# Down products of two experts on the two column halves of a PSUM bank, added by the turn, in a hybrid attention and expert kernel

## What is computed

```python
def _L2_ffn_ref(x, Wr, br, W1, b1, W2, b2, gamma, beta):
    ...
    logits = jnp.mean(x, axis=1) @ Wr + br
    routing_weights = jax.nn.softmax(logits, axis=-1)
    ...
    top_w, top_i = jax.lax.top_k(rw_tok, K)      # K = 2 of 8 experts, the same for a whole batch
    top_w = jax.nn.softmax(top_w, axis=-1)
    xf = x.reshape(N, D)
    h = jax.nn.gelu(jnp.einsum('nd,edf->enf', xf, W1) + b1[:, None, :], approximate=False)
    y = jnp.einsum('enf,efd->end', h, W2) + b2[:, None, :]
    w_dense = jnp.zeros((N, E), x.dtype).at[jnp.arange(N)[:, None], top_i].add(top_w)
    out = jnp.einsum('ne,end->nd', w_dense, y).reshape(B, S, D)
    out = _layer_norm(out + x, gamma, beta)
    return out
```

## Time and profile before

| | us |
|---|---|
| median of 3 runs | 166.78 |
| lowest, highest run | 165.62, 178.18 |
| the profiled execution's own time | 166.28 |
| its span, first to last instruction | 164.5 |
| PE busy | 146.8 |
| DVE busy | 110.5 |
| ACT busy | 75.5 |
| POOL busy | 51.2 |

### The profile page before, as it was taken

How to read it: one execution, slowest core, us unless ns; L and a number is a source line. 1 busy time by engine, 2 the same in 40 slices (tenths; PEclk the granted TensorE clock), 3 DMA queues, 4 the chain that set the end, 5 groups by cost and what they waited for, 6 DMA issues and landing times.

```text
span 164.5 us, 3153 instructions
## 1 busy us (share of the span) xinstructions
PE 146.8 (89%) x1087; PEld 102.8 (62%) x1087; DVE 110.5 (67%) x383; ACT 75.5 (46%) x198; POOL 51.2 (31%) x79
## 2 busy tenths in 40 slices
PE   7999977999999999799899999967999999899920
PEld 2598745578888887488454554445665746588520
DVE  2027663879778898752844638947969499696773
ACT  3455605314454445453154750397635842655140
POOL 7032459867655657410320032520003300000000
PEclk9999999599999999999999999999999999999985
DMA  5994035274550000027300000000000000000002
GB/s 144 356 421 117 4 108 116 80 196 135 138 132 2 6 0 0 4 78 243 147 0 0 0 0 4 0 2 0 2 0 0 4 0 0 0 0 4 0 0 66
DMA packets 7099, 10.31 MB, mean 63 GB/s; under 512 B 2720, under 2 KB 5609, under 8 KB 6699
## 3 DMA queue, kind: packets, MB, share of 16 engines
q1 hardware_dynamic: 6880, 9.72, 19.7%
q10 hardware_dynamic: 202, 0.38, 1.0%
HBM read 8.53 MB, written 1.57 MB: 61 GB/s over the span
## 4 chain that ended last, share of the span: by engine, by line
PE 69%; DVE 15%; ACT 7%; POOL 3%; issue 3%; DVEq 1%; ACTq 0%
PE bank L472 6%; PE bank L456 6%; PE bank L651 4%; PE bank L914 4%; PE bank L608 4%; PE bank L632 3%; PE bank L960 3%; PE bank L628 3%; PE bank L943 3%; PE bank L610 3%; PE bank L634 3%; PE bank L479 3%; PE bank L785 2%; PE bank L772 2%; PE bank L824 2%
## 5 line engine op out<-in xcount | busy, mean ns | idle before, releaser
L456 PE MATMUL bank<-onesb 128*128 128x512 bf16 x124 | 33.5, 412 | 1.0 <-DVE onesb L1294 1.0
L421 POOL TENSOR_TENSOR half_mem<-identb,nm 128x256 bf16<-128x256 bf16 x32 | 19.5, 614 | 12.5 <-DVE nm L1376 12.4
L456 PEld LDWEIGHTS bank<-onesb 128*128 128x128 bf16 x124 | 12.3, 107 | 13.9 <-issue 3.6
L1376 DVE TENSOR_REDUCE nm<-bank 128x2 bf16<-128x352 f32 x32 | 16.4, 517 | 5.0 <-PE bank L610 4.8
L1074 ACT ACTIVATE mid_mem<-mid_mem 128x352 f32<-128x352 f32 x20 | 9.8, 496 | 19.1 <-DVE mid_mem L1387 19.1
L628 PE MATMUL bank<-stack_mem 72*128 72x176 bf16 x64 | 13.7, 240 | 0.1
L634 PE MATMUL bank<-half_mem,onesb 128*128 128x176 bf16 x64 | 13.6, 239 | 0.0
L608 PE MATMUL bank<-stack_mem 72*128 72x176 bf16 x64 | 12.7, 241 | 0.3 <-DVE nm L1376 0.3
L610 PE MATMUL bank<-half_mem,identb 128*128 128x176 bf16 x64 | 12.6, 239 | 0.0
L1387 DVE TENSOR_TENSOR mid_mem<-bank,bias_mem 128x352 f32<-128x352 f32 x20 | 10.3, 542 | 0.0
L632 PE MATMUL bank<-bias_mem,identb 128*128 128x176 bf16 x72 | 9.3, 238 | 0.0
(11 more groups left out here) (287 smaller groups left out, 335.7 us busy)
## 6 DMA issues: line engine op xcount, KB each, us to landing
stack_mem<-qk_parts SPq DMA_DIRECT2D x21, 96.0 KB
bias_mem<-bias_q SPq DMA_DIRECT2D x1, 1408.0 KB, 8.7
bias_mem<-bias_k SPq DMA_DIRECT2D x1, 1408.0 KB, 12.4
mid_mem<-w SPq DMA_DIRECT2D x1, 1024.0 KB, 7.4
qk_parts<-half_mem SPq DMA_DIRECT2D x4, 192.0 KB, 2.6
qk_parts<-half_mem SPq DMA_DIRECT2D x4, 128.0 KB, 2.4
mid_mem<-w2b SPq DMA_DIRECT2D x1, 512.0 KB, 8.1
Cs<-cst SPq DMA_DIRECT2D x1, 340.0 KB, 4.2
```

The source lines that it names most:

```text
L421: pool.tensor_tensor(diag1[:, b % 2, h, :].rearrange("p (q k) -> p q k", q=TB), identb[:, :].unsqueeze(1).to_broadcast([P, TB, P]), nm1[:, ...
L456: pe.matmul(idle[:, :].rearrange("p (k q) -> p k q", k=4), onesb[:, :], onesb[:, :].unsqueeze(1).to_broadcast([P, 4, P]), start=True, stop ...
L1376: dve.tensor_reduce(nm1[:, n // NH, n % NH, :], bank[n % 2][:, 0:TB * SPAN].rearrange("p (q k) -> p q k", q=TB), AX.X, ALU.max, negate=Tru ...
```

## The change

The two down products of a batch no longer accumulate. Expert k's product goes to partitions 64 k to 64 k + 63 of the bank, as a group of its own. The bias add reads and writes all 128 partitions; `UT` and `b2sel` grow from 64 to 128 partitions, and the lower half of `b2sel` is set to zero once, at the program's start, on DVE. The turn is no longer a transpose: it is a matmul of `UT` (128 x 128 as weights) with the constant `Cs[:, CST["twice"]]`, two 64 x 64 unit matrices one above the other, which turns and adds the two halves in one go. The number and order of the instructions are unchanged on PE, ACT, POOL and SP; DVE has one more, the memset.

```diff
-        b2sel = sb("b2sel", [C, B])
+        b2sel = sb("b2sel", [P, B])
...
-        UT = half_mem[0:C, IOTA_AT + SLOTS:IOTA_AT + SLOTS + B * N]
+        UT = half_mem[:, IOTA_AT + SLOTS:IOTA_AT + SLOTS + B * N]
...
                     for k in range(TOPK):
-                        last = pe.matmul(bank[4 + b % 2][0:C, 0:N], W2sel[:, TOPK * b + k, :],
-                                         H2[:, b, k * N:k * N + N], start=(k == 0), stop=(k == TOPK - 1))
+                        last = pe.matmul(bank[4 + b % 2][k * C:k * C + C, 0:N], W2sel[:, TOPK * b + k, :],
+                                         H2[:, b, k * N:k * N + N], start=True, stop=True, skip_group_check=True)
                     last.then_inc(sem("down2"), 1)
...
                     for q in range(TB):
-                        last = pe.transpose(bank[6 + b % 2][:, q * C:q * C + C], UT[:, b * N + q * P:b * N + q * P + P],
-                                            ident[0:C, 0:C])
+                        last = pe.matmul(bank[6 + b % 2][:, q * C:q * C + C], UT[:, b * N + q * P:b * N + q * P + P],
+                                         Cs[:, CST["twice"]], start=True, stop=True)
                     last.then_inc(sem("u_turned"), 1)
...
             dve.memset(share[:, :], 1.0 / N).then_inc(sem("onesb"), 1)
+            counted(dve.memset(b2sel[C:P, :], 0.0))
             dve.wait_ge(sem("weights_p"), 2)
...
-            dve.tensor_reduce(b2sel[:, :], b2w[:, :, :].rearrange("p (b k) e -> p b (k e)", b=B), AX.X, ALU.add) \
+            dve.tensor_reduce(b2sel[0:C, :], b2w[:, :, :].rearrange("p (b k) e -> p b (k e)", b=B), AX.X, ALU.add) \
                 .then_inc(sem("b2sel"), 1)
...
-                    dve.tensor_scalar(UT[:, b * N:b * N + N], bank[4 + b % 2][0:C, 0:N], b2sel[:, b:b + 1],
+                    dve.tensor_scalar(UT[:, b * N:b * N + N], bank[4 + b % 2][:, 0:N], b2sel[:, b:b + 1],
                                       None, ALU.add) \
                         .then_inc(sem("ut"), 1)
```

## The result

| | before | after |
|---|---|---|
| median of 20 runs each, us | 167.52 | 165.75 |
| lowest run, us | 165.24 | 164.02 |
| ratio of the times, 95% interval | | 0.9945 (0.992 to 0.997) |
| profiled execution, us | 166.28 | 165.85 |
| its span, us | 164.5 | 164.0 |

The changed kernel is faster by 0.55%, between 0.3% and 0.8%. The ratio leaves the disturbed runs of both kernels out, which is why the two medians (1.1% apart) are not used. The forecast of 165.3 us is 0.45 under the measured median and its range holds it.

A forecast was written before the change was run, and what follows sets the result against it. PE alone was taken to bound the second feed-forward from 91.40 to 99.23 us. Down-product savings less turn costs bring add 2 1.05 us earlier: 166.28 - 1.05 = 165.23, forecast 165.3 us, range 164.0 to 167.2.

The forecast's parts named there:

- The down products: Second feed-forward on PE: passes to the two partition halves run in pairs, a stage 0.58 instead of 1.01 us, saving 0.43 each.
- The turn: Behind the down products on PE: four passes replace two; turn 0 +0.19, turn 1 +0.29, turn 2's result 0.32 us later.
- The stage: Second feed-forward, from down 0's first weight load to add 2's start (D, 7.20 us before): add 2 comes 1.05 us earlier.
- The added memset, held to be covered: DVE, ahead of the Wvo copy: hidden in 4.32 us of idling; uncovered, no more than 0.22 us.
- the last step: From stage gain to verdict: 2% (3.3 us) needed to tell a change; faster 0.04, same 0.92, slower 0.04.
- No overlap: Rival, down stages: the halves run one after the other, only the turns count, 166.9 us; chance 0.05.
- loads in line: Rival, down stages: second-half loads wait for the pass on the same rows, 0.4 us in all, 165.6 us; chance 0.06.
- The turn at a transpose's price: Rival, turns on PE: they cost what transposes do, only the down products count, 1.7 us gained, 164.6 us; chance 0.06.
- Absorbed: Rival, behind the stage: something later does not move, likeliest the keep-warm block holding L804, 166.3 us; chance 0.06.
- The falling clock: Rival, behind down 1: PE streams less and drops to 1.2 GHz, up to 1.7 us later, 166.9 us; chance 0.07.

The follow-up runs named there:

- The early keep-warm matmuls alone: The token halves with more keep-warm matmuls ahead of the second layer's projections (3, 5, 10 instead of 2, 4, 6): median 165.97 us, ratio 0.989.
- both sets together: The token halves with those early matmuls and 4 instead of 1 in the last layer-norm: medians 164.59 and 164.49 us, ratios 0.988 and 0.990.
- the token halves: Changed kernel with bank halves holding tokens instead of experts, products accumulating again, turn one transpose: ratio 0.989 against the kernel before, first profile 163.12 us.

## Why the prediction was right or wrong

**The down products** were right: 0.58 us a stage where 0.58 was worked out, 0.43 saved each. The row of L977 carried over, both for the pairing and for the loads. The loads of both halves, on the same rows, take 0.20 us for four and are over at 93.12, while the passes of the stage hold the chain until 93.57. The rule of the Trainium skill ("TensorE: Matmul & The Clock Gate", Part 3) that loads overlap with running matmuls only where the row groups differ does not hold here, and the measurement decides.

**The turn** was right in size: 0.44 for turn 0 (0.45), 0.59 for turn 1 (0.56), the result of turn 2 at 99.10 - 98.40 = 0.70 after its start (0.66 + 0.04). In the stage it costs 0.68 when it is put in alone: 0.18 in turn 0, 0.32 in turn 1 and 0.18 in front of add 2. The doubled turns, at 0.45 each, confirm its size and that it lies on the chain.

**The stage**: D 6.18, a gain of 1.02 where 1.05 was forecast. Turn 2 took the place of bias add 3 as what add 2 waits for, as said. The gain went through to L804 (add 2 to L804: 8.62 before, 8.64 after) and to the end. The added memset, held to be covered, was: it runs at 2.00 us, and the copy behind it still waits 4.63 us for PE.

**What was wrong** is the last step, from the stage to what can be measured. I wrote that about 2% (3.3 us) is what a measurement of this kernel can tell from no change, and gave no row for it. With twenty runs each the interval is 0.25% either way, and a change of 0.55% is more than twice that, so it stands clear of no change. That bound alone turned a worked-out gain of 1.05 us into "same", with a chance of 0.92, and this is the step that failed: the kernel is faster, by about what the sum said. The mechanism would have carried a plain "faster by 0.6%".

The absolute time was a second, smaller miss. I set the sum against one profiled execution and called the result 165.3. The executions of one kernel differ outside the stage: two profiles of the changed kernel by 0.49 us ahead of down 0 alone (92.92 and 92.43), and groups of its runs by 1 to 2 us. The low stretch near 30 us does not explain the 0.45, since the profile of before has it (0.58 from 28.8 to 32.9 us) as well as that of after (0.70). The 0.46 that the profile of after lost at the start is of the right size; that the median run lost it too is not shown.

**The rivals.** No overlap and loads in line are out, by the stage's 0.58. The turn at a transpose's price is out, by the new turn alone. Absorbed is out: add 2 to L804 is 8.62 and 8.64. The falling clock did not happen where the rival put it: in the profiles of the changed kernel PE is granted 1.00 throughout the stage, and the falls are near 30 us and at the end. In some of the other versions there are more, near 130 us, and in the profile of the paired products without their turn one ahead of the stage (clock 0.57 from 86 to 90 us, down 0 at 94.85). So the mechanism is one of this kernel, and none of these profiles has it in the stage.

What stays open: why the low clock comes near 130 us in one execution and not in another of the same kernel. The early keep-warm matmuls alone did not narrow the spread of six runs, both sets together did, in 18 runs; whether the late ones do it alone, and how many of the three are needed, was not tried.

## What to carry to other kernels

Where a product fills only 64 of 128 output partitions, the other half can carry a second one: four stages went from 1.01 to 0.58 us each here. A line of the same kernel that already used both halves gave the price to a hundredth. Choose what is split over the halves so that nothing has to be added later: splitting experts bought 1.69 us and paid 0.68 back in the turn; splitting tokens gained 2.01, with a turn no dearer than before. Measure such a change between two fixed instructions of the profile, since the run's time carries steps as large as the effect, and take many runs before calling it nothing.

## What was not expected of the hardware

The loads of two separate matmuls, one for each half, overlap: four of 0.13 us are done in 0.20, and eight in 0.42. Eight passes of 128 columns (0.59 us) cost the same as four of 256 (0.58). The same kernel, the token halves, has a span of 161.3 or 163.5 us, by one stretch at 1.2 GHz (clock 0.51 from 127 to 134 us); both kinds of run, near 163.1 and near 165.7, also occur within one set of twelve. And six added matmuls in idle time ahead of 28 us did not remove the steps between runs, while these six with three more on the chain near 126 us, at 0.6 us, narrowed the runs from 163.1 to 167.9 us down to 163.7 to 165.5 (leaving out those near 178).
